# Row maxima of two attention layers moved between stages of a fused two-layer kernel

## What is computed

```python
Q = _split_heads(x, H)
K = _split_heads(x @ Wk + bk, H)
V = _split_heads(x @ Wv + bv, H)
scores = jnp.einsum('bhqd,bhkd->bhqk', Q, K) + mask
attn = jax.nn.softmax(scores, axis=-1)
o = jnp.einsum('bhqk,bhkd->bhqd', attn, V)
return x + jax.nn.gelu(o, approximate=False) @ Wf + bf
```

```python
gm = jax.nn.one_hot(sel, EXPERTS, dtype=x.dtype) * gates
values = jnp.einsum('bhne,ehdk,bnd->bhnk', gm, value_experts, x)
attn = jax.nn.softmax(sim, axis=-1)
out = jnp.einsum('bhij,bhjk->bhik', attn, values)
out = jnp.einsum('bhne,ehkd,bhnk->bhnd', gm, output_experts, out)
```

## Time and profile before

| | |
|---|---|
| Median of 3 runs | 1350.18 us (1346.76 to 1360.11) |
| The profiled execution | 1347.51 us, its span 1345.8 us |
| Busy share: PE, ACT, DVE, POOL | 86%, 72%, 65%, 23% |
| Mean granted TensorE clock | 0.951 |
| Matmuls / DVE / ACT instructions | 5720 / 2725 / 2671 |

### The profile page before, as it was taken

One profiled execution on the slowest core, in us unless ns is written; L12 is line 12 of the kernel. 1 busy time (PEld: TensorE's weight loads), 2 busy tenths in 40 slices (PEclk: granted clock), 3 DMA queues, 4 the chain that ended last, 5 costly groups with the idle time before them and its releaser, 6 DMA issues.

```text
span 1345.8 us, 19795 instructions
## 1 busy us (share of the span) xinstructions
PE 1160.4 (86%) x5720; PEld 634.3 (47%) x5720; DVE 872.1 (65%) x2725; ACT 967.8 (72%) x2671; POOL 306.1 (23%) x418
## 2 busy tenths in 40 slices
PE   2797898898888989899888989889898898989998
PEld 1126643366424754247433564336642475434653
DVE  4625757577574866758576585756758486764845
ACT  3894777948597686966779577795779767696660
POOL 1023311232102411133112231123220241112220
PEclk8567999999999999999999999999999999989999
DMA  6211240022300323003320124102240032300310
GB/s 184 65 66 33 51 123 20 4 64 67 109 2 4 80 79 81 2 11 72 105 55 2 45 50 112 37 4 64 59 114 4 4 80 77 83 2 3 72 48 24
DMA packets 43644, 72.71 MB, mean 54 GB/s; under 512 B 9664, under 2 KB 25408, under 8 KB 43216
## 3 DMA queue, kind: packets, MB, share of 16 engines
q1 hardware_dynamic: 38416, 54.67, 15.0%
q10 hardware_dynamic: 5120, 16.78, 4.8%
HBM read 45.34 MB, written 8.80 MB: 40 GB/s over the span
## 4 chain that ended last, share of the span: by engine, by line
PE 38%; ACT 27%; DVE 15%; issue 12%; DMA 5%; POOL 2%; SPq 2%; ACTq 0%; DVEq 0%; POOLq 0%
ACT masked L838 13%; ACT pt L895 9%; PE ps_m L624 7%; PE ps_o L615 6%; DVE masked L1153 4%; PE ps_exp L441 3%; PE ps_max L721 2%; DVE pt L1304 2%; PE ps_exp L531 2%; PE ps_m L441 2%; PE ps_exp L443 2%; DMA s2q<-mt_f 2%; PE ps_exp L442 2%; PE ps_m L443 2%; PE ps_m L442 2%
## 5 line engine op out<-in xcount | busy, mean ns | idle before, releaser
L1153 DVE CUSTOM_DVE_ANT_0 masked<-ps_max,mask 128x512 f32<-128x512 f32 (+3 forms) x768 | 353.5, 487 | 207.9 <-PE ps_max L529 100.0
L838 ACT ACTIVATE masked<-masked,low 128x512 f32<-128x512 f32 (+3 forms) x768 | 426.1, 558 | 65.5 <-DVE low L1153 62.2
L895 ACT ACTIVATE pt<-ps_exp 128x384 f32<-128x384 f32 (+1 forms) x480 | 247.7, 523 | 95.7 <-PE ps_exp L532 75.6
L1036 POOL TENSOR_SCALAR_AFFINE_SELECT pt<-pt 128x512 f32<-128x512 f32 (+2 forms) x192 | 133.3, 695 | 697.3 <-ACT pt L895 697.3
L624 PE MATMUL ps_m<-at,oe_sb 128*128 128x512 f32 x416 | 220.7, 620 | 5.6 <-DVE at L1204 3.5
L615 PE MATMUL ps_o<-pt,val 128*32 128x128 f32 (+6 forms) x1536 | 191.9, 476 | 12.1 <-POOL pt L1036 11.6
L529 PE MATMUL ps_max<-s2k,s1q 72*128 72x512 bf16 (+3 forms) x512 | 141.8, 326 | 34.4 <-DMA s2k<-onesb_d 21.9
L1204 DVE TENSOR_TENSOR at<-osb,hots 128x512 f32<-128x512 f32 x208 | 145.3, 705 | 15.5 <-PE ps_m L624 15.5
L838 ACT ACTIVATION_READ_ACCUMULATOR masked<-masked,low 128x1 f32 x768 | 149.7, 195 | 0.0
L529 PE MATMUL ps_exp<-s1q,s2k 75*128 75x384 bf16 (+3 forms) x384 | 104.9, 324 | 44.0 <-ACT pt L895 41.5
L531 PE MATMUL ps_exp<-s1q,s1k 128*128 128x256 f32 (+2 forms) x256 | 100.1, 402 | 19.9 <-DMA s2q<-mt_f 19.7
(11 more groups left out here) (170 smaller groups left out, 1919.0 us busy)
## 6 DMA issues: line engine op xcount, KB each, us to landing
hots<-hot_d ACTq DMA_DIRECT2D x64, 256.0 KB, 4.1
s1q<-parts_q SPq DMA_DIRECT2D x96, 96.0 KB
s2k<-parts_k SPq DMA_DIRECT2D x96, 96.0 KB
s1q<-pt SPq DMA_DIRECT2D x64, 128.0 KB, 2.3
s1k<-pt SPq DMA_DIRECT2D x64, 128.0 KB, 2.3
parts_q<-pt SPq DMA_DIRECT2D x24, 128.0 KB, 2.3
parts_k<-pt SPq DMA_DIRECT2D x24, 128.0 KB, 3.0
x_sb<-in_x SPq DMA_DIRECT2D x8, 256.0 KB, 2.8
```

Source lines behind the costliest of these rows:

```text
L838: last = nc.scalar.activation(e, e, ACT.Exp, bias=low[:, g % 2, c:c + 1], scale=-1.0, accum_out=den[:, g % 2, c:c + 1])
L895: nc.scalar.activation(pt[:, (n % 2) * 4 + j, 0:c1 - c0], score_bank(k, u)[:, c0:c1], ACT.Exp).then_inc(exp_done[k].sem, 1)
L1036: nc.gpsimd.affine_select(out=v, in_=v, compare_op=ALU.is_ge, fill=0.0, base=0, pattern=[[0, HG[k]], [0, m], [1, P]], channel_multiplier=- ...
L1153: last = v.tensor_tensor_reduce(out=masked[:, u % JUNK, c0:c0 + w], in0=src[:, c0:c0 + w], in1=mask[:, S - w:S], scale=-1.0, scalar=POS, o ...
```

## The change

Five things move; apart from where they stand, every instruction stays, except that two copies change engine.

1. Layer F's twelve first maximum units stand behind the expert values 12, 13, 15, 16, 18, 19, 21, 22, 24, 25, 27 and 28. The negation goes from value 27 to 23 and the transpose from 30 to 25. ACT takes its part of a unit within the expert stage, one value later, and copies group 0's transposed maxima at value 25. ACT copies the low halves of k of the pairs 2 and 3 ahead of the plain expert values.
2. `FIRST` has two units of layer A at each of layer F's units 12 to 23: groups 0 and 1. Group 0's negation stands at unit 21, its transpose at 23 and ACT's copy of it at layer F's end.
3. In layer A of batches 1 to 7 group 2 stands ahead of the first score unit in place of group 1, and group 3's twelve units are spread over the score units 2 to 22 (`LATE`). Batch 0 does groups 0, 1 and 2 ahead.
4. `PREP` makes k two units later in layer F (3 to 6). ACT copies layer A's V tiles 1 and 3, with a semaphore of their own, `vb`.
5. In `turn` one output product goes ahead of the back projection, and the others move up by one.

```diff
-MAX_FROM, NEGATE_AT, TRANSPOSE_AT = 20, 27, 30
+NEGATE_AT, TRANSPOSE_AT, COPY_AT = 23, 25, 25
 N_MAX = 2 * STAGES * HG["F"]
-MAX_AT = {MAX_FROM + n: range(N_MAX * n // (T * E - MAX_FROM), N_MAX * (n + 1) // (T * E - MAX_FROM))
-          for n in range(T * E - MAX_FROM)}
+MAX_AT = {12 + 3 * m // 2: (m,) for m in range(N_MAX)}
...
-FIRST = {FIRST_AT + n: (n,) for n in range(STAGES * HG["A"])}
+A_UNITS = STAGES * HG["A"]
+FIRST = {FIRST_AT + n: (2 * n, 2 * n + 1) for n in range(A_UNITS)}
+LATE = {2 + 11 * n // 6: n for n in range(A_UNITS)}
+NEGATE_A, TRANSPOSE_A = 21, 23
+def pre_groups(a):
+    return (0, 1, 2) if a == 0 else (2,)
...
-PREP = {"q1": 0, "q2": 0, "K": 1, "k0": 1, "k_rest": 2, "k1": 3, "k2": 4}
+PREP = {"q1": 0, "q2": 0, "K": 3, "k0": 3, "k_rest": 4, "k1": 5, "k2": 6}
...
-                    dst = free("A", "V", t, (va, a, t + 1))
+                    dst = free("A", "V", t, ((va, vb)[t % 2], a, t // 2 + 1))
...
                             score_unit("A", a, g, s, j)
-                            if g + 2 < GROUPS:
-                                max_unit("A", a, g + 2, s * HG["A"] + j)
+                            if u in LATE:
+                                if LATE[u] == 0:
+                                    pe.wait_ge(restacked_a[3].sem, restacked_a[3].count(a, 16 * RESTACK["A"]))
+                                max_unit("A", a, 3, LATE[u])
...
-                                for m in FIRST.get(u, ()):
-                                    max_unit("A", f + 1, 0, m)
+                                for first in FIRST.get(u, ()):
+                                    g_a, m = divmod(first, A_UNITS)
+                                    if m == 0:
+                                        pe.wait_ge(restacked_a[g_a].sem, restacked_a[g_a].count(f + 1, 16 * RESTACK["A"]))
+                                    max_unit("A", f + 1, g_a, m)
+                                if u == TRANSPOSE_A:
+                                    maxima_transposed("A", f + 1, 0)
...
                 f, first = a - 1, T * E - TURN
+                if f >= 0:
+                    product(f, first + 1)
                 project_back(a, (0, 1, 2))
                 if f >= 0:
-                    product(f, first + 1)
+                    product(f, first + 2)
                 project_back(a, (3,))
...
+            def values_a(a):
+                for t in range(1, T, 2):
+                    act.wait_ge(v_ready.sem, v_ready.count(a, t + 1))
+                    copy(val[:, t], ps_m[BANK[("A", "V", t)]][:]).then_inc(vb.sem, 1)
...
+                    for p in {5: (2,), 7: (3,)}.get(u, ()):
+                        kl = pt[:, 4 * (p % 2) + 3].bitcast(F32R)
+                        act.wait_ge(qk_lo.sem, qk_lo.count(f, 2 * p + 2))
+                        for odd in range(2):
+                            copy(s2k[ROWS[odd], 2 * p + odd], kl[ROWS[odd]]).then_inc(s2k_made.sem, 1)
...
+                            for m in MAX_AT.get(n - 1, ()):
+                                denominators("F", f, *divmod(m, STAGES * HG["F"]))
+                                if m == STAGES * HG["F"] - 1:
+                                    logs("F", f, 0)
+                            if n == COPY_AT:
+                                maxima("F", f, 0)
...
-                for t in range(T):
+                for t in range(0, T, 2):
                     dve.wait_ge(v_ready.sem, v_ready.count(a, t + 1))
                     v.tensor_copy(val[:, t], ps_m[BANK[("A", "V", t)]][:]).then_inc(va.sem, 1)
```

More of the change, by code:

```diff
@@ L642, in attention_a @@
                 n_units = STAGES * HG["A"]
-                for g in range(2):
-                    if g == 0 and a > 0:
-                        continue
+                for g in pre_groups(a):
                     pe.wait_ge(restacked_a[g].sem, restacked_a[g].count(a, 16 * RESTACK["A"]))
@@ L913, in attention @@
                     if b + 1 < B:
-                        for first in FIRST[NST * HG[k] - 1]:
-                            denominators("A", b + 1, 0, first)
-                        logs("A", b + 1, 0)
+                        firsts(b + 1, NST * HG[k] - 1)
+                        maxima("A", b + 1, 0)
             def turn(a):
@@ L1218, in attention_a @@
                 n_units = STAGES * HG["A"]
-                if a > 0:
-                    negate("A", a, 0)
-                for g in range(2):
-                    if g == 0 and a > 0:
-                        continue
+                for g in pre_groups(a):
                     for n in range(n_units):
```

55 lines of the change are left out of this document (33 added, 22 removed).

## The result

| | before | after |
|---|---|---|
| Median | 1353.1 us (20 runs, 1345.3 to 1360.1) | 1361.7 us (20 runs, 1353.8 to 1377.8) |
| Ratio to before, 95% interval | | 1.0079 (1.0053 to 1.0104) |
| A second set of runs of the same file, `again` | 1350.0 us (7) | 1369.5 us (4), 1.016 (1.0117 to 1.0202) |
| Span of the profiled execution | 1345.8 us | 1368.9 us (`again`) |
| Busy share: PE, ACT, DVE, POOL | 86%, 72%, 65%, 23% | 86%, 72%, 63%, 22% |

The account below looks back on a forecast made before the run. The bound changes by stage: ACT in layer A's first half, PE in layer F's second, PE and DVE in experts. Seven batches at -3.3 plus eight at -2.2 give -40.7 us: 1308 us, range 1284 to 1338.

Parts of the forecast that it names:

- late k at +0.4 us: Layer F's first half: k restack issued 0.4 us later, PE waits +0.4 us more a batch (0 to +1.5).
- F's second half, +4.3 us: Layer F's units 12 to 23 take twelve more maximum units: 22.9 to 27.2 us a batch (+2.4 to +8.7).
- the share of 0.93: Busy share assumed where two engines are equally full, from PE's 12.09 of 13.00 us in the stage behind layer A's first half.
- An ACT chain in layer F: Rival: layer F's scores wait for exponentials behind two maximum units; +8.7 in place of +4.3, 1322 to 1345 us, chance 0.2.
- Layer A's first half, -7.2 us: Score groups 0 and 1, bound by ACT, lose twelve maximum units: 29.2 to 21.9 us a batch (-5.6 to -8.9).
- From V to the first exponential: V's start to ACT's first layer A exponential, V copies split between DVE and ACT: -0.8 us a batch (0 to -1.5).
- F's start, -2.2 us: ACT's maxima finish under PE's expert work, so layer F starts 2.2 us sooner in all eight batches (-1.0 to -3.2).
- the bound of 1 us: Expert stage: PE's end stays when the maximum units are spread; the move costs 0, between -1 and +1 us.
- The turn: A product fills PE's 0.86 us wait for gelu, but the back projection's end doesn't move: 0 (to -0.4).
- The late restack at unit 18: Rival: group 1's restack lands 0.9 us after unit 18 starts, 6 us in all; with other gain-eating waits, chance 0.08.
- ahead of the first gelu: Startup: ACT's two V copies (1.4 us at DVE's price) fall where ACT sits idle, so 0.

Follow-up runs that it names:

- best1_old_turn: Changed kernel with k made at units 1 to 4, gate tables 1 and 2 at stages 7 and 9, DVE copying all V tiles, the turn as before: 1308.4 us, 0.9668.
- before_hots: Kernel before with only gate tables 1 and 2 made and sent later, at layer F's stages 7 and 9: 1336.6 us, 0.989 of before.
- groups_only: Kernel before with only layer A's maxima moved a group sooner (parts 2 and 3 of the change): 1340.8 us, 0.991 of before.
- row_first: Changed kernel, k still late, with SP sending group 2's row of maxima ahead of group 0's q restack: 1364.2 us, 1.012 of before.
- k_early: Changed kernel with only the move of k undone (made at units 1 to 4 as before): 1327.3 us, 0.984 of before.
- best2: Changed kernel with k early, gate tables at stages 7 and 9, DVE's four V copies, group 0's k restack ahead of the row: 1313.5 us, 0.9718.
- hots_later: Changed kernel, k still late, with the second and third gate tables moved to units 14 and 18: 1338.6 us, 0.995 of before.
- k_early_hots: Changed kernel with k made at units 1 to 4 and the gate tables' transfers later: 1311.8 us, 0.975 of before.

## Why the prediction was wrong, point by point

**The step that failed: late k at +0.4 us.** The prediction said that SP "has its own idle there: 653.15 plus 2.27, then nothing until 658.01", so that the k restack goes out 0.4 us later and PE waits that much more. Measured, late k costs 6.0 us a batch in the changed kernel and 5.4 in the kernel before; its bound had been 1.5. That idle was the gap that let the restack's transfers drain ahead of the row of maxima. I priced issues on SP, took landing times as fixed, and looked only at what PE waits for at 664.53, not at its wait for the row 1.5 us ahead of that. The row goes out nearly as early as before, but now directly behind the restack and together with ACT's 512 KB of gate tables, and takes 7.63 us to land instead of 4.27. Moving the tables takes back 3.1 of the 4.7 us in F's first half. F's second half grew by 1.3 us with it. Seven times 5.6 us too little is 39 us, most of the 54 by which the forecast missed the median of 1361.7.

**F's second half, +4.3 us.** At full clock it is 25.4 us in `best1_old_turn` against 21.3 in `before_hots`: +4.1, and PE is busy for 23.82 of the 25.40, close to the share of 0.93 that I had taken. In part that is luck: I had put ACT's 25.3 us over this share, with 9.3 more than before, and ACT's busy time within these marks grew by 7.5 us only (15.42 to 22.94), so the fuller engine is PE, with 3.0 us more. And the earlier trace rows had shown two levels for this stage, 24.50 at clock 0.87 and 22.90 at 1.00, and I took the fast one for the sum. The changed order meets the slow one in most batches: +5.6 in `groups_only`, +5.0 in the three kernels with k early and the tables where they were, +6.3 in the changed kernel. "An ACT chain in layer F" is not what made it longer: ACT is busy 23.80 of 29.30 us there and PE 28.13.

**Layer A's first half, -7.2 us.** From layer A's first exponential to its twenty-sixth it took 29.1 to 30.8 us before, and it takes 22.9 us in six of seven batches of `groups_only`, and 22.9 to 24.6 (mean 23.7) in `again`, the longer ones where the clock falls within it. So the forecast of 21.9 was 1 to 2 us too low and the gain 6.4 in `again`. The rest of layer A, up to gelu, then took 14.8 to 15.3 us instead of 14.1 to 14.5, which the prediction didn't have. From V to the first exponential it was -1.0 without the split and -0.5 with it; -0.8 was forecast for the split, which costs 0.5 by itself. Together -6.2 in the changed kernel, -7.2 in `groups_only`, against -8.0 in the sum.

**F's start, -2.2 us.** -1.4 at the q copy and -0.7 within F's first half. The q copy now starts 0.1 us behind the end of PE's transposes, where it was 2.1 to 2.4 us, as forecast. But PE's end of the expert stage didn't stay: the last transpose starts 53.1 us behind gelu, where it was 52.5, within the bound of 1 us that the prediction gave the move. ACT's first exponential comes 21.5 us ahead of the q copy instead of 12.7, about the forecast 10 sooner.

**The turn and the rest.** 0 as forecast. The late restack at unit 18, the mechanism that I had set on the slower side, didn't come: `again` has no wait for a restack in layer F. The slower side came by the term that I had called nearly free.

Without its late-k term the sum would have been 7 x -3.7 - 17.6 = -43.5 us for the kernel with k early. That measured -22.7 by its median, and -20.1 from span to span of the profiled executions. The missing 23 us of the spans are layer A (1.7 in seven, 12 us), F's second half (0.7 in seven, 5 us), F's start (3 us, as batch 7 gained nothing from gelu to its end), and 4 us ahead of the first gelu (105.1 us against 101.3), where the prediction had 0. These 4 us can't be put down to the change: `row_first` has the same start as `k_early` and comes to its first gelu at 100.0. The granted clock is at 0.50 for 54.6 us there and for 78.5 us in `k_early`.

**Still open.** What decides whether TensorE's clock falls in F's second half. In `k_early` PE waits twice within some 2 us, 0.4 to 1.4 us for the row and 0.4 to 1.4 for the restack, and the clock falls in six of seven batches. In `best1_old_turn` the wait for the row is gone, the one for the restack is 0.8 to 1.2 us, and it falls in none. But in `best2` PE has one wait of 1.2 us for DVE, and it falls in six. And what is left of late k in F's second half when the tables are out of the way (1.9 us, `hots_later` against `k_early_hots`) was measured, not taken apart. Nor does a run show why the restack and the tables together hold the row back so much longer than either does.

## What to carry to other kernels

Before you call a stage's slack free, ask what ends it. A queue's idle stretch ahead of a small, urgent transfer can be what lets the large ones ahead of it drain: a transfer has a landing time besides its issue, and here it depended on what both queues had issued in the microseconds before: 4 KB needed 7.6 us where 4.3 had been enough. And where a stage shows two durations at two clocks, make the sum with both, not with the faster one.
